# Moving the loads of `enc` and of half of `W` between two DMA queues, and putting GpSimd's first eight gathers in one row

## The reference

```
x = x + ffn0(mix(x, W0c[kind0]))      # kind0: one of 16 per sample
x = x + ffn1(mix(x, W1c[kind1]))      # kind1: one of 32 per sample

mix(x, w)   = einsum('bct,bcd->bdt', x, w)             # 32x32 for each sample, picked by its kind
ffn0(z)     = z @ W_base.T + b_base
              + 0.5 * sum over 3 experts of fourier((z @ enc.T) @ (coefs * mask).T)   # enc: 40 x 512
ffn1(y)     = scale * (y @ (2 * kernel - 1))           # kernel: 512 x 512 of 0 and 1
fourier(c)  = an orthogonal inverse real Fourier transform over 512
```

## Time and profile before

| | |
|---|---|
| median of 3 runs | 214.99 us (214.96 to 215.11) |
| the profiled execution | 215.02 us |
| its span, first to last instruction | 213.2 us |
| TensorE's granted clock | 1.00 of full speed |
| busy in the span: PE, DVE, ACT, POOL | 97%, 57%, 59%, 52% |

### The profile page before, as it was taken

The page is one execution under the profiler, slowest core; times in us unless marked ns, Lnnn a source line. Parts: engine busy times, 40 slices in busy tenths (PEclk is TensorE's granted clock), DMA queues, the critical chain, the costliest instruction groups (busy, mean ns, idle before and its releaser), DMA issues.

```text
span 213.2 us, 4965 instructions
## 1 busy us (share of the span) xinstructions
PE 207.3 (97%) x1636; PEld 197.1 (92%) x1636; DVE 122.1 (57%) x219; ACT 125.2 (59%) x398; POOL 111.5 (52%) x134
## 2 busy tenths in 40 slices
PE   7898999999999999999999999999999999999994
PEld 3787999999999999999999999999999999999994
DVE  5664855545665555566655555665555466655553
ACT  3566865555677555556765555676655556765630
POOL 5758766655545665555456655455665555621300
DMA  6991044433334444323344443334444333331112
GB/s 183 388 342 31 9 161 155 151 119 119 128 107 154 154 151 152 124 87 130 125 154 153 151 150 99 118 102 150 154 151 154 109 121 119 116 148 51 52 49 98
DMA packets 18043, 28.60 MB, mean 134 GB/s; under 512 B 2890, under 2 KB 5194, under 8 KB 18034
## 3 DMA queue, kind: packets, MB, share of 16 engines
q1 hardware_dynamic: 15360, 26.56, 36.4%
q0 software_dynamic: 2048, 1.05, 2.2%
q10 hardware_dynamic: 626, 0.87, 1.2%
HBM read 20.09 MB, written 8.39 MB: 134 GB/s over the span
## 4 chain that ended last, share of the span: by engine, by line
PE 90%; DMA 3%; ACT 2%; issue 2%; another core or an unknown queue 1%; DVE 1%; ACTq 1%; DVEq 0%
PE z_ps L582 38%; PE a_ps L639 14%; PE f_ps L648 13%; PE f_ps L653 13%; PE f_ps L624 7%; PE f_ps L628 3%; DMA w_sb<-in_L_ffn_W_base 3%; ACT a_high L366 1%; PE a_ps L653 0%; PE a_ps L648 0%; ACTq L299 0%; PE a_ps L568 0%; DVE x L476 0%; DVE xt_low L429 0%
## 5 line engine op out<-in xcount | busy, mean ns | idle before, releaser
L245 POOL DMA_INDIRECT gathered<-in_L_cond_weights,row_now x56 | 54.8, 979 | 13.0 <-issue 8.8
L470 DVE TENSOR_TENSOR y_low<-a_ps,y_high 128x512 fp32r<-128x512 f32 x32 | 22.1, 691 | 64.7 <-ACT y_high L342 64.7
L342 ACT ACTIVATE y_high<-a_ps 128x512 fp32r<-128x512 f32 x32 | 19.2, 600 | 65.2 <-issue 46.4
L582 PE MATMUL z_ps<-a_high,xt_high 128*128 128x256 f32 (+1 forms) x230 | 50.2, 290 | 0.1
L582 PE MATMUL z_ps<-a_low,xt_high 128*128 128x256 f32 x256 | 49.9, 277 | 0.0
L252 POOL TENSOR_TENSOR x<-x_in,bias 128x512 f32<-128x512 f32 x32 | 40.9, 1279 | 15.5 <-DVE xt_low L429 9.8
L582 PE MATMUL z_ps<-a_high,xt_low 128*128 128x256 f32 (+1 forms) x225 | 47.2, 303 | 0.0
L582 PEld LDWEIGHTS z_ps<-a_low,xt_high 128*128 128x128 f32 x256 | 40.4, 188 | 2.3
L582 PEld LDWEIGHTS z_ps<-a_high,xt_high 128*128 128x128 f32 x230 | 38.2, 188 | 2.9 <-issue 0.5
L639 PE MATMUL a_ps<-blocks,x 128*128 128x128 f32 x256 | 33.8, 275 | 1.1 <-DVE x L476 1.1
L323 ACT ACTIVATE blocks<-mix_parts 32x64 fp32r<-32x64 f32 x128 | 32.5, 254 | 3.1
(11 more groups left out here) (65 smaller groups left out, 175.6 us busy)
## 6 DMA issues: line engine op xcount, KB each, us to landing
xt_in<-in_x_t SPq DMA_DIRECT2D x32, 256.0 KB
x_in<-in_x SPq DMA_DIRECT2D x32, 256.0 KB
out_x<-x SPq DMA_DIRECT2D x31, 256.0 KB
gathered<-in_L_cond_weights,row_now POOLq DMA_INDIRECT x56
w_sb<-in_L_ffn_W_base SPq DMA_DIRECT2D x2, 256.0 KB, 4.6
w_sb<-in_L_ffn_W_base ACTq DMA_DIRECT2D x2, 256.0 KB
basis_sb<-in_fourier_basis ACTq DMA_DIRECT2D x2, 129.0 KB, 3.0
bias<-in_L_ffn_b_base SPq DMA_DIRECT2D x1, 256.0 KB
```

Of the source, the lines that this page charges most:

```text
L245: nc.gpsimd.indirect_dma_start(gathered[:, slot, layer, :], None, mix_rows[layer], IndirectOffsetOnAxis(rows[:, layer:layer + 1].bitcast(u ...
L470: nc.vector.tensor_tensor(out=y_low[:, slot % PAIR, :], in0=y_ps[slot % PAIR][:, :], in1=y_high[:, slot % PAIR, :].bitcast(f32), op=ALU.su ...
L582: last = nc.tensor.matmul(z_ps[slot % PAIR][:, columns], xt[:, slot % PAIR, k * P:(k + 1) * P], a[:, k, columns], start=(start and half == ...
```

## The change

`enc` is loaded by SP, between `packed` and the first piece of `W_base`, into a tile of exactly 40 rows. ACT issues pieces 2 and 3 of `W_base` right behind the basis, ahead of its first activation. GpSimd no longer clears the `enc` tile before its load but the whole of `enc_parts`, so it is ACT's conversion that waits for the clearing and no longer ACT's DMA. The conversion and the subtraction go over 40 partitions in place of 64. GpSimd issues all eight gathers of the first four tiles in a row and adds the bias of tiles 0 and 1 behind them; its waits for `a_low_ready` and `xt_low_ready` are gone.

```diff
-        enc_sb = sb("enc_sb", [ENC_LOW, T], f32)
+        enc_sb = sb("enc_sb", [R, T], f32)
...
         def _(sp):
             for rows, rows_in, loaded in zip(packed, (sines_in, cosines_in), packed_loaded):
                 sp.dma_start(rows[:, :], rows_in).then_inc(loaded, 16)
+            sp.dma_start(enc_sb[:, :], enc).then_inc(enc_loaded, 16)
             load_w(sp, 0)
             load_w(sp, 1)
...
         def _(pool):
-            nc.gpsimd.memset(enc_sb[0:ENC_LOW, :], 0.0).then_inc(enc_zero, 1)
+            nc.gpsimd.memset(enc_parts[:, :].bitcast(f32), 0.0).then_inc(enc_zero, 1)
...
             pool.wait_ge(row_of_ready, 1)
-            gather(row_of[:, 0, :], 0)
-            gather(row_of[:, 1, :], 1)
+            for slot in range(RING):
+                gather(row_of[:, slot, :], slot)
             pool.wait_ge(bias_loaded, 16)
-            pool.wait_ge(a_low_ready, 1)
             add_bias(0, 0)
-            gather(row_of[:, 2, :], 2)
-            gather(row_of[:, 3, :], 3)
-            pool.wait_ge(xt_low_ready, 3)
             add_bias(1, 0)
...
         def _(act):
             for side in range(2):
                 act.dma_start(basis_sb[:, side, :, :], basis[side]).then_inc(basis_loaded[side], 16)
-            act.wait_ge(enc_zero, 1)
-            act.dma_start(enc_sb[0:R, :], enc).then_inc(enc_loaded, 16)
+            load_w(act, 2)
+            load_w(act, 3)
             act.wait_ge(idle_zero, 1)
             nc.scalar.activation(warm[:, :], idle[:, :], ACT.Copy)
-            load_w(act, 2)
-            load_w(act, 3)
...
             negate(0)
+            act.wait_ge(enc_zero, 1)
             act.wait_ge(enc_loaded, 16)
-            nc.scalar.activation(enc_parts[0:ENC_LOW, :], enc_sb[:, :], ACT.Copy).then_inc(enc_high_ready, 1)
+            nc.scalar.activation(enc_parts[0:R, :], enc_sb[:, :], ACT.Copy).then_inc(enc_high_ready, 1)
...
-            nc.vector.tensor_tensor(out=enc_parts[ENC_LOW:, :], in0=enc_sb[:, :], in1=enc_parts[0:ENC_LOW, :].bitcast(f32),
+            nc.vector.tensor_tensor(out=enc_parts[ENC_LOW:ENC_LOW + R, :], in0=enc_sb[:, :], in1=enc_parts[0:R, :].bitcast(f32),
                                     op=ALU.subtract).then_inc(enc_low_ready, 1)
```

## The result

| | before | after |
|---|---|---|
| median, us | 214.88 (213.97 to 215.20, 8 runs) | 216.98 (215.65 to 218.41, 8 runs) |
| profiled execution, us | 215.02 | 215.8 |
| its span, us | 213.2 | 213.9 |

The ratio is 1.009 (95% interval 1.007 to 1.011): the change makes the kernel 0.9% slower. The eight times after lie in groups: 215.65, 215.8 and 215.82; 216.87 to 217.44, four times; one of 218.41. The granted clock in the four near 217 is that of the lowest group (0.999 to 1.000), so it is not what parts them. The profile is of an execution of the lowest group.

What follows compares the result with a forecast made beforehand. TensorE, busy 207.3 of 213.2 us, was taken as the bound, with room only before 11.88 and at 19.71 to 20.76 us. Only the W_base load counted: 215.02 - 0.13 = 214.89, so 214.9 us, range 213.7 to 215.5.

Steps and rivals of the forecast that it cites:

- The gathers in a row: GpSimd's gathers 5 to 8 follow number 4 directly, ending at about 15.4 us; cost nothing.
- Nobody waits: Gathered rows: ACT takes tile 2's only behind tile 0's mix1 at 20.76, so early gathers delay no engine.
- a late signal from TensorE: At 17.90: reading of the 2.02 us wait, as ACT and VectorE were released together at about 20 us.
- Rival one: Ahead of tile 0's residual0: wait at 17.90 goes, winning TensorE's 1.05 us; 213.8 us, chance 0.18.
- The bias additions behind them: GpSimd's additions for tiles 0 and 1 end at about 16.7 and 18.0; cost nothing.
- the price is nothing, with 0.3 us to spare: Second bias addition beside VectorE's xt_low of tile 2: if held, it ends at 18.7, before TensorE's use at 18.98.
- Piece 1 of `W_base`: Load on SP's queue: lands at 8.05, first sum at 9.55 in place of 9.68; gain 0.13 us.
- piece 1 is late: SP's load of W_base: landing at 9.0 puts the first sum at 10.5, time 215.8 us; chance 0.17.
- Nothing that GpSimd or a DMA does there can move the time: From 26 to 206 us: TensorE is busy for 180.00 of 180.00 us, so changes there have no effect.
- `enc` earlier: Head: enc on SP's queue lands up to 0.86 us earlier, transposes may begin 0.4 to 0.5 us earlier.

Runs made afterwards that it cites:

- gathers_only: Kernel before with only the change's GpSimd list (eight gathers in a row, bias additions behind), loads as before; 216.87 us, ratio 1.0094.
- two_landed_two: Kernel before, but GpSimd waits until tile 2's gathered rows have landed before issuing tile 3's two gathers; 215.00 us, ratio 0.9987.
- bias_between: four_biases_two_two with the third bias addition put between the gathers of tiles 4 and 5; 213.90 us, ratio 0.9962 to the kernel before.
- order2301: Changed kernel with TensorE transposing the pieces of W_base in the order 2, 3, 0, 1; 216.84 us, ratio 1.0094 to the kernel before.
- after_again: The changed kernel measured once more, nothing altered; 215.88 us, ratio 1.007 to the kernel before.
- loads_only: Kernel before with the change's loads of enc and W_base, GpSimd's gathers and additions as before; 215.21 us, ratio 1.002.
- pairs_all: Kernel before with GpSimd's gathers for the first four tiles issued in pairs, separated by waits, both bias additions ahead of tile 2's; 215.25 us, ratio 1.0011.
- pairs_landed: pairs_all with GpSimd also waiting for rows to land after tile 2's and tile 3's gathers; 222.11 us, ratio 1.034 to the kernel before.
- eight_bias_late: Eight gathers in a row, loads as before, the two bias additions waiting for xt_low_ready 2 and 3; 215.83 us, ratio 1.004 to before.
- six_then_two: Kernel before with tile 2's gathers issued ahead of the first bias addition, so six in a row; 215.22 us, ratio 0.9989.
- four_biases_two_two: Kernel before with the second bias addition ahead of tile 2's gathers and tile 3's gathers waiting for x1_ready 1; 214.35 us, ratio 0.9989.
- four_biases_at_once: four_biases_two_two without the wait between the two bias additions; 214.55 us, ratio 0.9991 to the kernel before.

## Why the prediction was wrong

The time was forecast at 214.9 with a range to 215.5, and slower by over 0.2% had 0.17; it is 0.9% slower. Point by point:

- **The gathers in a row** are the step that failed: "Nobody waits". The term stood at nothing; alone it measured 2.0 us at the median (`gathers_only`, 216.87 for 214.86): some 0.7 us in the executions near 215.6, and 1.3 more in those near 216.9. The reasoning asked who uses the gathered rows, and it was right that nobody misses them. It did not ask what else happens while GpSimd issues them. During a long row TensorE's signals are held up, and the engines that wait for TensorE start late. The chain of the kernel before already showed one such wait (2.02 us at 17.90), the prediction read it as "a late signal from TensorE" and stopped there, "whose list has not changed". It stood over the row of gathers 5 to 8 all the same, and the change moved that row and made it twice as long.
- **Rival one**, that this wait goes away, was half right: it did go, but because the row now lay under feed0 of tile 0, whose signal was held in its place. Where it is taken away for good, TensorE's 1.05 us go (from 12 to 30 us it is busy for 18.00 of 18.00 in `two_landed_two` and `bias_between`). The median gained about a microsecond in `bias_between`, whose list differs in more than that, and only 0.17 in `two_landed_two`. The cause that the rival gave, the second bias addition, was not the one: in `bias_between` `z_high` of tile 0 starts at 15.61, 0.10 us behind its matmuls, beside an addition that runs from 15.39.
- **The bias additions behind them**: "the price is nothing, with 0.3 us to spare". The lock was weighed for `xt_low` of tile 2. What it caught in `order2301` was `mix_parts` and with it `xt_low` of tile 1, when the additions stood back to back and VectorE was late. TensorE waited 1.79 us for it. This is shown for one execution of the second group of that kernel. That the four times near 217 of the changed kernel are the same is not shown: no execution of them was profiled, and the group gets rarer with the additions apart (2 of 10 for 15 of 26) but does not go.
- **Piece 1 of `W_base`**: forecast to give a first sum at 9.55, 10.1 at worst; it was 10.52 in the profile, at the place that "piece 1 is late" gives (10.5), and that rival's 215.8 is the profiled time to the digit. It is a coincidence. `after_again`, the same kernel, had the sum at 9.87, inside the forecast, and took 215.83; `gathers_only` had it at 9.33 and took 215.54. The term was mis-sized all the same: alone the loads cost 0.35 us (`loads_only`), where a gain of 0.13 was forecast. Under the eight gathers they cost nothing that can be seen, since `z_high` starts at 17.1 to 17.2 anyway.
- **"Nothing that GpSimd or a DMA does there can move the time"**, said of 26 to 206 us because TensorE was busy all through, holds only while GpSimd keeps its lead. With the gathers put off, TensorE was busy there for 177.56 of 180.00 us in `pairs_all` and for 173.22 in `pairs_landed`.
- **`enc` earlier** was right: conversion at 5.01 for 5.72, the second cosine product at 6.50 for 6.88; it moved nothing behind it, since `W_base` was not there.
- The gathers were to end at about 15.4 and the additions at 18.0, with SP's load at about 16.7: 15.90, 18.45 and 17.25. No idle time of TensorE from 26 us on: right.

How late the signals are, worked out from the timelines as start of the waiting engine less end of the matmuls:

| kernel | gathers in the row over it | last issue ends | matmuls end | waiter starts | late by | behind the row |
|---|---|---|---|---|---|---|
| before | 4 | 18.79 | 18.33 | 20.02 (VectorE) | 1.69 | 1.23 |
| loads_only | 4 | 19.07 | 18.60 | 20.19 (VectorE) | 1.59 | 1.12 |
| gathers_only | 8 | 15.82 | 14.43 | 17.11 (ACT) | 2.68 | 1.29 |
| after | 8 | 15.90 | 15.34 | 17.18 (ACT) | 1.84 | 1.28 |
| after_again | 8 | 15.63 | 14.69 | 17.22 (ACT) | 2.53 | 1.59 |
| eight_bias_late | 8 | 16.29 | 15.41 | 17.40 (ACT) | 1.99 | 1.11 |
| order2301 | 8 | 15.41 | 15.96 | 17.17 (ACT) | 1.21 | 1.76 |
| six_then_two | 6 | 12.96 | 10.98 | 14.15 (ACT) | 3.17 | 1.19 |
| four_biases_two_two | 6 | 29.08 | 27.73 | 28.45 (ACT) | 0.72 | -0.63 |
| four_biases_at_once | 6 | 28.29 | 27.08 | 29.09 (ACT) | 2.01 | 0.80 |
| pairs_all | 8 | 29.14 | 26.97 | 30.03 (ACT) | 3.06 | 0.89 |
| two_landed_two | none | | 18.61 | 18.71 (VectorE) | 0.10 | |
| pairs_landed | none | | 27.10 | 27.14 (ACT) | 0.04 | |
| bias_between | none | | 27.43 | 27.46 (ACT) | 0.03 | |

The row was moved to five places and the late signal went with it, to 0.8 to 1.8 us behind the last issue in all but one (`four_biases_two_two`, ahead of it). That the row of gathers makes TensorE's signals late is shown. How it does so is open. It is not the issuing alone: in `order2301` the last issue ended 0.55 us ahead of the matmuls, and the signal was late all the same. The end of the gathers' own packets in the traces fits better: they end at 19.74 in the kernel before, 17.19 after, 16.87 in `gathers_only`, 17.28 in `order2301` and 16.69 in `after_again`, and the waiting engine starts within 0.3 us of that (0.5 behind it in `after_again`). No run was made to test it, and it doesn't fit throughout: in `six_then_two` ACT started at 14.15, and they ended at 16.40. The matmuls themselves are on record as done, the semaphore is raised late, and nothing in the profile shows what lies between. The Trainium skill ("Perfetto Trace Analysis", Summary: the profiler window per engine type) says of TensorE that the end in the record is an estimate and the way of its signal is hidden; so whether the last matmuls or only their signals were late can't be told here.

## What to carry to other kernels

A wait that the profile can't name ("another core or an unknown queue", "remote") had its cause in the same kernel here, as only one core was at work: look what the engines that are not on the path do at that moment, and whether it goes when that is moved. Don't put GpSimd's indirect DMAs in one long row beside work that hands over from engine to engine; spread them out with other GpSimd work between, and give them no longer a row later for being put off now. Put an addition on GpSimd beside VectorE's operations that read PSUM, not beside those with both operands in SBUF.

## What was not expected of the hardware

- In long rows of indirect DMAs on GpSimd the engines that wait for TensorE start up to 3.2 us behind the matmuls' recorded end (0.7 to 3.2 in the table); where no long row lay over it, the same handover took 0.03 to 0.10 us (the last three rows of the table). Not every signal in a row is held (in the kernel after, that of the first sum was taken up 0.04 us behind it, at 11.26, in the middle of the eight), and no length is a clear limit: four in a row held it in the kernel before (14.05 to 18.79), and a row of four later (20.07 to 26.09, `bias_between`) did not.
- The same loads brought the first sum at 9.33, 9.68, 10.30 and 10.59 us in four executions (`gathers_only`, before, `two_landed_two`, `bias_between`), and the loads of the change at 9.87 and 10.52 in two of one kernel: a difference of half a microsecond in the head can't be read from one profile.
